# When the first attention period turns its latents, and which early steps carry filler matmuls and weight splits

## The reference

```python
x = x + attn(lstm(x, cond))          # 16 heads, keys and values from a 32-wide latent, causal
x = x + moe(gru(x, cond))            # 8 experts of width 512, top 2 of 8
# lstm: a = x_t Wx + h Wh + b;  c = f c + i g;  h = o tanh(c)
# gru:  z, r, candidate; after each 4th step h = tanh(h Wp + bp)
```

## Time and profile before

| | us |
|---|---|
| time, median of 3 runs | 546.38 (544.72 to 546.54) |
| the profiled execution, time | 542.14 |
| its span in the profile | 540.4 |
| PE busy | 508.1 (94% of the span) |
| DVE busy | 435.9 (81%) |
| ACT busy | 364.7 (67%) |
| TensorE clock granted, mean share of full | 0.97 |

### The profile page before, as it was taken

The page is one execution under the profiler, slowest core; times in us unless marked ns, Lnnn a source line. Parts: engine busy times, 40 slices in busy tenths (PEclk is TensorE's granted clock), DMA queues, the critical chain, the costliest instruction groups (busy, mean ns, idle before and its releaser), DMA issues.

```text
span 540.4 us, 20477 instructions
## 1 busy us (share of the span) xinstructions
PE 508.1 (94%) x7464; PEld 468.7 (87%) x7506; DVE 435.9 (81%) x2370; ACT 364.7 (67%) x1329; POOL 34.6 (6%) x89
## 2 busy tenths in 40 slices
PE   7988889898799999999999999999999999889997
PEld 3756666898689999999999999999999998879986
DVE  4567888789878888888888888898888888865785
ACT  2355645875467767677777777676767677776995
POOL 7000010100000000001010101010000001000010
PEclk9799999999769999999999999999999999979999
DMA  8910102010101011110101010101010111100000
GB/s 212 366 18 7 20 2 23 2 19 11 21 3 16 9 15 16 16 12 12 19 14 16 7 18 15 21 3 19 15 16 8 14 16 16 12 1 1 13 6 13
DMA packets 75121, 14.35 MB, mean 27 GB/s; under 512 B 71412, under 2 KB 74112, under 8 KB 74639
## 3 DMA queue, kind: packets, MB, share of 16 engines
q1 hardware_dynamic: 74566, 11.96, 12.3%
q10 hardware_dynamic: 456, 1.08, 0.7%
HBM read 7.78 MB, written 1.05 MB: 16 GB/s over the span
## 4 chain that ended last, share of the span: by engine, by line
PE 78%; DVE 10%; ACT 6%; issue 4%; SPq 1%; DMA 1%; POOL 0%; ACTq 0%; DVEq 0%; POOLq 0%
PE pH L516 19%; PE pY L516 13%; PE pG L516 12%; PE pL L516 9%; PE pC L516 7%; PE pV L516 7%; PE pC L608 6%; PE pS L516 5%; ACT hid L912 2%; ACT PThi L901 1%; SPq L436 1%; DVE w1lo L1189 1%; DVE ghi L1233 1%; DMA gscale<-in_gscale 1%; ACT P L895 1%
## 5 line engine op out<-in xcount | busy, mean ns | idle before, releaser
L912 ACT ACTIVATE hid<-pH,b 128x256 f32<-128x256 f32 (+1 forms) x320 | 115.1, 449 | 0.0
L516 PE MATMUL pY<-w,hid 128*128 128x128 f32 (+1 forms) x656 | 80.9, 268 | 0.0
L516 PE MATMUL pH<-ghi,w1hi 128*128 128x256 f16 (+1 forms) x320 | 76.0, 254 | 2.3 <-ACT hid L912 1.7
L516 PE MATMUL pH<-ghi,w1lo 128*128 128x256 f16 (+1 forms) x320 | 76.3, 255 | 0.0
L516 PE MATMUL pH<-glo,w1hi 128*128 128x256 f16 (+1 forms) x320 | 76.3, 255 | 0.0
L516 PEld LDWEIGHTS pY<-w,hid 128*128 128x128 f32 (+1 forms) x656 | 70.5, 171 | 0.1
L923 ACT ACTIVATE gT<-pG 128x32 f32<-128x32 f32 x128 | 24.9, 194 | 54.8 <-PE pG L516 52.8
L901 ACT ACTIVATE PThi<-pC 128x512 f16<-128x512 f32 x64 | 38.1, 596 | 22.0 <-PE pC L608 21.8
L516 PE MATMUL pG<-gRZ,gW 128*128 128x16 f32 x256 | 45.6, 254 | 4.2 <-DVE gRZ L1206 3.9
L516 PEld LDWEIGHTS pG<-gRZ,gW 128*128 128x128 f32 x256 | 40.0, 196 | 8.0 <-DVE gRZ L1206 6.8
L516 PEld LDWEIGHTS pL<-hhi,lWhi 128*128 128x128 f16 x512 | 42.1, 116 | 5.4 <-DVE hhi L1250 4.6
(11 more groups left out here) (188 smaller groups left out, 1641.0 us busy)
## 6 DMA issues: line engine op xcount, KB each, us to landing
w<-in_w SPq DMA_DIRECT2D x2, 2048.0 KB, 13.7
qbd<-qh SPq DMA_DIRECT2D x256, 16.0 KB, 1.9
out<-acc SPq DMA_DIRECT2D x16, 64.0 KB, 1.6
xT<-in_xT ACTq DMA_DIRECT2D x1, 960.0 KB, 7.9
hid<-in_WqT SPq DMA_DIRECT2D x1, 512.0 KB, 5.4
hid<-in_Wout SPq DMA_DIRECT2D x1, 512.0 KB, 9.9
lWh<-in_lWh SPq DMA_DIRECT2D x1, 256.0 KB, 2.8
lWx<-in_lWx SPq DMA_DIRECT2D x1, 256.0 KB, 3.3
```

Of the source, the lines that this page charges most:

```text
L516: return nc.tensor.matmul(o, lhsT=lhsT, rhs=rhs, start=start, stop=stop, skip_group_check=True)
L912: A(hid[:, e % NHID, c, 0:W], pH[half][:, W * at:W * (at + 1)], ACT.Gelu, bias=b1[:, e, c:c + 1], scale=1.0 / SP).then_inc(gelu, 1)
```

## The change

It does four things. The turn of the first period's latents moves from steps 9 (high) and 10 (low) to steps 11 and 12. The fillers at the ends of steps 11, 12, 13, 14 and 16 go (twice two in each; steps 15 and 17 had none there). The low turn of the second period moves from step 18 to 19. The weight split of expert 0 moves from step 18 to 19; the table then has experts 0 and 1 at step 19, 2 and 3 at step 24, and expert 4 at step 25, which had none.

```diff
-W1_LO = {18: (0,), 19: (1, 2), 24: (3, 4), 26: (5, 6), 27: (7,)}
+W1_LO = {19: (0, 1), 24: (2, 3), 25: (4,), 26: (5, 6), 27: (7,)}
...
-                if k < WARM_END and k != LAG - 1 and t % GS != GS - 1:
+                if k < WARM_END and not TB + O_S < k < LAG and t % GS != GS - 1:
                     keep_warm(k, startup_fill(k))
                 if unit_at(k, O_S) is not None and k >= LAG:
                     scores(unit_at(k, O_S), k)
-                if k < LAG and k != LAG - 1 and t % GS != GS - 1:
+                if k <= TB + O_S and t % GS != GS - 1:
                     keep_warm(k, startup_fill(k))
...
-                if k % TB == 1 and TB < k <= T + 1:
+                if k % TB == (3 if k < LAG - 1 else 1) and TB < k <= T + 1:
                     turn_latents(k // TB - 1, lathi, latNhi)
-                if k % TB == 2 and TB < k < LAG:
+                if k % TB == 4 and TB < k < LAG:
                     turn_latents(k // TB - 1, latlo, latNlo)
...
-                if k % TB == 2 and LAG <= k <= T + 2:
+                if k == LAG + 1 or k % TB == 2 and LAG < k <= T + 2:
                     turn_latents(k // TB - 1, latlo, latNlo)
```

## The result

The changed kernel is slower, by a little. Its median is 544.95 us (543.66 to 546.69, 22 runs), that of the kernel before in the same series 543.20 us (541.10 to 548.13, 22 runs). The ratio is 1.0033, with a 95% interval of 1.0018 to 1.0047: +1.8 us, between +1.0 and +2.6. The three runs shown ahead of the prediction (546.38) lay high. Later comparisons added 134 runs of the kernel before; over these its mean is 543.0 us, and over its 22 runs the mean of the changed kernel is 545.0.

What follows compares the result with a forecast made beforehand. PE was taken to bound the kernel, busy nearly throughout. Fillers -0.2, steps 18 and 19 +0.1, step 25 +0.26 gave +0.2 us; a clock fall added 1.0: +1.2 on 546.38, so 547.6 us, range 544.2 to 549.9.

Steps and rivals of the forecast that it cites:

- half a per cent: Whole kernel: 2.7 us, about what a measurement can tell from no change; chance 0.76 of landing within, between 543.7 and 549.1.
- I take 0.9 to 1.1 for the likeliest: Clock fall somewhere in steps 12 to 14: costs 0.9 to 1.1 us, ending before the period fill of step 15.
- the 0.9 of the prediction: Step 13 at the low clock: four transposes and two fillers before ACT's copy run slower, costing 0.9 us more.
- case C: Rival: the fall comes late or lasts through step 15's period fill and step 17's projection; +3.2 us, 549.6; chance 0.15.
- B: The forecast itself: a clock fall that ends before the period fill; +1.2 us, 547.6; chance 0.43.
- At the full clock, the fillers: Removed fillers, steps 11 to 16: steps 11 to 13 give nothing, 14 to 16 give 0.2; -0.2 us, bounds 0 and -1.7.
- The first turns: First period's turns in steps 11 and 12: low one delays lP of step 13 some 0.2 us, covered, costs nothing.
- Steps 18, 19 and 25: Moved split and low turn, between gA and gB: -0.5 in step 18, +0.61 in 19; +0.26 from step 25's split.
- The split and the second period's turn: Whole move from step 18: net +0.1 us for steps 18 and 19, and +0.26 for step 25.
- the sum at the full clock: All edits without a clock fall: -0.2 + 0.1 + 0.26 = +0.2 us, that is, nothing.
- A: Rival: the clock holds without the removed fillers; +0.2 us, 546.6; chance 0.27.
- D: Rival: chain of waits right at face value for fillers of steps 13, 14 and steps 18, 19; -2.3 us, 544.1; chance 0.15.

## Why the prediction was right and wrong

I forecast +1.2 us by a fall of the clock in steps 12 to 14. The fall is there. The loss is about 1.8 us by the medians and 2.0 by the means, 0.33%. That is inside the half per cent to which I had given 0.76. But I had called half a per cent about what can be told from no change, and that was wrong: over 22 runs of each kernel the interval is 0.15% to either side, and the loss is clear of zero.

**The step that failed** is the term "I take 0.9 to 1.1 for the likeliest", with the ground given for it, that the wide matmuls of step 15 bring PE's load back. It counted one fall of some 7 us. The first fall was of that kind: 6.8 us in the profile, 0.85 us between the scores of unit 2 and ACT's copy for the 0.9 of the prediction, and the period fill of step 15 at 1.40 as I had it. But the runs carry 10.5 us more at the low clock on the mean, and the profiled one a second fall of 10.2 us at 55.4. From lP of step 17 to step 20 it lost another 2.2 us. I had the stage of steps 15 to 17 as case C, with 0.15. What came is neither C nor B: the clock is back for step 15 and goes again behind the few matmuls of step 17. The GRU's fill at 55.65, which no term of mine named, then runs at half speed. So the mechanism was right, and the size of this term was too small by 0.6 to 0.8 us on the mean and by more in the profiled run. Why the clock goes a second time stays open.

**At the full clock, the fillers.** The scores of unit 1 came at 37.52 (said: 37.7) and those of unit 2 at 41.55 (said: 41.2), with a longer wait in front, 1.97 us. In the kernel with extra fillers there unit 2 did not come later either. The 0.4 us of unit 2 are a later landing of its transfer, for which I had no term. For steps 14 to 16 I had said -0.2. In the kernel with the fillers in the waits, where the clock holds, lP falls back by 0.10 us up to step 14 and gains 0.28 by step 16, which leaves the 0.2. lT of step 17 comes another 0.66 us earlier there, as the four fillers of step 16 are gone, but lP of step 17 waits for DVE as before and gains nothing. That piece was covered, as said.

**The first turns** I had at nothing. The low turn delays lP of step 13 by 0.5 us and not 0.2 (in the kernel with only these turns moved, against its shift at step 11), but this is covered, as said. In the changed kernel lP of step 13 stands right behind the low turn, and ACT's copy comes 2.6 us later:

```profile
40.55 0.69 DVE L1042 STREAM_TRANSPOSE latNlo<-latlo 32x512 f16<-32x512 f16 x1
41.18 0.14 DVE L1239 SCALAR_TENSOR_TENSOR lP<-lT 128x32 f32<-128x32 f32 x1
```

But the argument took the transfers of unit 2 to land as before, and in the profiles with moved turns they land later. The mean over the runs (542.6 us) shows no cost and would hide one of 0.5 us.

**Steps 18, 19 and 25.** I had -0.5, +0.61 and +0.26; alone they measured -0.47, +0.59 and +0.09. The last was over-sized. gRZ of step 26 has lost its wait, as said, and more of the 0.60 hides than that:

```profile
87.72 0.19 DVE L1206 SCALAR_TENSOR_TENSOR gRZ<-gT,g 128x32 f32<-128x32 f32 x1
```

The split and the second period's turn (+0.2) and steps 14 to 16 (-0.2) add up to nothing, so the loss is the clock's, apart from what the later transfer may cost. The fillers' removal alone takes 1.5 us (544.5 against 543.0), and their return gives back 1.8 (545.0 to 543.2).

**The rivals.** A, the clock holds, is out: the kernel before has 33.4 us at the low clock, the changed one 43.9. D, the chain at face value, is out: where the clock held without the 20 fillers (those in the waits), lP came ahead by 0.28 us at most. The chain names them because PE was doing them while the transfers landed.

The Trainium skill (TensorE: Matmul & The Clock Gate, the table on why this matters for your kernels) asks for no long idle gaps between bursts. By that rule the sum at the full clock would have stood. The trace does not agree. Ahead of the fall at 38.3 PE's longest wait was 1.52 us (the scores at 37.52), and PE was busy for 1.88 of 3.40 us. The same page (Part 4: PE-mode transpose) says that a transpose does not count for the gate in the same way; no run here shows that alone.

**What stays open.** How the clock's time turns into the kernel's. Over the later runs of the kernel before, a line through span and time at the low clock gives 0.31 us for each us of it, if one run is left out whose clock (0.93) is far below the others at a usual span; with it, 0.19. The changed kernel has 10.5 us more and takes 2.0 us more, which is 0.19. Which falls an execution gets is not settled either. A fall that begins between 37 and 39 us is in all five profiles of kernels that lack the end fillers of steps 11 to 13 and have no wide ones in the waits, and in none of the twelve others, though one of these falls at 43.0. The second fall does not follow the fillers so. Falls of 3.4 us between 61 and 68 us are in two profiles without fillers, but also in that with the fillers back, that with only the first turns moved, and two with fillers in the waits. All five profiles with the first turns moved have a fall between 55 and 81 us, and four of the twelve others; whether the turns have a part in it was not tried.

## What to carry to other kernels

A filler on the chain of waits need not be worth its length. Ask first what ends just behind it, and then what the clock does without it, by comparing the stretch with the thinnest ones of the same trace. A change that thins PE's work is judged by the time at the low clock over many runs, since one profile shows one draw of the falls. If fillers are wanted, put them in front of an instruction that waits for a transfer, where they were free here up to the length of the wait. In front of one that sets the step two of them cost 0.35 of their 0.43 us.

## What was not expected

- **The spread of the kernel before goes with its clock.** Its first 22 runs range over 7 us. Of the 134 later ones, those with a mean clock of 0.975 have spans of 539.2 to 540.2 us, and those with 0.959 have 544.0 to 545.4. Part of it is drawn before the first step that any edit touches: at step 8 the profiled executions are up to 2.0 us apart, and the fall that begins at about 20 us lasts 6.8 us in some and 10.2 in others.
- **Wide fillers and narrow ones did not do the same, in either place.** Four fillers of 8 columns in each step left the first fall where it was without fillers (37.6 to 44.4) and 42.0 us at the low clock, where wide ones in the waits came to 33.3. Two in each of steps 36 to 45 left 33.4, where wide ones came to 28.0.
- **The second fall does not keep to the fillers.** The kernel without the fillers of steps 14 and 16 shows none in its profile, and 35.9 us on the mean. The changed kernel with every filler back shows one.
- **A transfer came later with the turns moved.** In the profile of the changed kernel unit 2's scores stand 6.76 us behind those of unit 0, against 6.08 before. Where only the first turns were moved it is 6.92, where only the fillers went 6.20. The five profiles with moved turns have 6.49 to 6.92, eleven of the twelve others 6.00 to 6.55, and one 6.72. SP's last two transfers of unit 2 and the first of unit 3 land so in the changed kernel (least, median and longest, and the issue); the 3.6 is the last of unit 2:

```profile
DMA to landing us min/median/max: 1.9/3.1/3.6
...
37.24 1.92 SPq L436 DMA_DIRECT2D qbd<-qh  x3
```

The longest was 2.9 before. What delayed the transfer was not tried.
